# Moving the transposing loads and the output writes of a feed-forward stage from ScalarE's DMA queue to SyncE's

## The reference

```python
# attention-like part: a gated linear scan
params = einsum('btc,dc->btd', x, W) + b
gates, values = split(params, 2, axis=-1)
_, hidden = associative_scan(lambda a, b: (b.g*a.g, b.g*a.v + b.v),
                             (sigmoid(gates), tanh(values)), axis=1)
# feed-forward part, weights made ternary: {-1, 0, 1} * mean|w|
h = square(relu(einsum('bsd,hd->bsh', x, ternarize(w_fc))))   # H = 5120
y = einsum('bsh,dh->bsd', h, ternarize(w_proj))               # D = 2048
# the layer
x = x + layernorm(scan_part(layernorm(x)))
x = x + layernorm(ffn_part(layernorm(x)))
```

## Time and profile before

| | us |
|---|---|
| median of the 2 runs shown | 5565.78 |
| the two runs | 5473.66 and 5657.90 |
| the profiled execution, device time | 5452.77 |
| the profiled execution, span of the slowest core (core 2) | 5451.2 |
| spans of the eight cores | 5438.5 to 5451.2 |
| TensorE busy with matmuls, core 2 | 3681.0 (68%) |
| ScalarE busy | 1327.7 (24%) |
| VectorE busy | 1291.4 (24%) |
| GpSimd busy | 101.2 (2%) |

### The profile page before, as it was taken

The page is one execution under the profiler, slowest core; times in us unless marked ns, Lnnn a source line. Parts: engine busy times, 40 slices in busy tenths (PEclk is TensorE's granted clock), DMA queues, the critical chain, the costliest instruction groups (busy, mean ns, idle before and its releaser), DMA issues.

```text
span 5451.2 us, 57166 instructions; the slowest of 8 cores (5438.5 to 5451.2 us)
## 1 busy us (share of the span) xinstructions
PE 3681.0 (68%) x20742; PEld 2111.9 (39%) x20742; DVE 1291.4 (24%) x1830; ACT 1327.7 (24%) x2801; POOL 101.2 (2%) x140
## 2 busy tenths in 40 slices
PE   0004656068888889332695994986959949869897
PEld 0001222067777778331242442432424424324343
DVE  0466555022222322565002002011020020110101
ACT  0004666123333332000211302213113022131221
POOL 0000011000000000000000000000000000000000
PEclk9999999999999999655797996988979979989898
DMA  9787775722222221797445445444454454444443
GB/s 122 227 298 256 259 271 221 159 95 90 93 94 95 89 94 60 261 312 266 154 152 195 146 151 174 150 166 165 151 196 148 151 172 153 172 162 153 172 151 143
DMA packets 314431, 918.22 MB, mean 168 GB/s; under 512 B 220848, under 2 KB 220976, under 8 KB 229168
## 3 DMA queue, kind: packets, MB, share of 16 engines
q1 hardware_dynamic: 204976, 604.16, 32.4%
q0 software_dynamic: 21632, 192.95, 11.5%
q10 hardware_dynamic: 87552, 117.46, 6.5%
HBM read 704.76 MB, written 192.94 MB: 165 GB/s over the span
## 4 chain that ended last, share of the span: by engine, by line
PE 59%; DMA 11%; DVE 10%; ACT 7%; issue 5%; ACTq 3%; another core or an unknown queue 2%; SPq 2%; DVEq 0%; POOLq 0%
PE ps_pj L902 20%; PE ps_fc L889 20%; PE ps_par L550 15%; DMA x_sb<-x 4%; ACTq L811 3%; DMA wslab<-wfc 3%; DVE st6c L46 3%; DMA wslab<-wpj 2%; PE ps_bf L353 2%; ACT stage_pj L374 2%; PE ps_bf L345 2%; ACT stage_fc L367 1%; DMA x1a_sb<-x_s 1%; DVE st6a L46 1%
## 5 line engine op out<-in xcount | busy, mean ns | idle before, releaser
L889 PE MATMUL ps_fc<-xn1T_sb,sfc_sb 128*128 128x512 bf16 x5120 | 1133.3, 385 | 436.2 <-ACT r_sb L823 351.1
L550 PE MATMUL ps_par<-xnT_sb,wt_sb 128*128 128x256 bf16 x8192 | 935.1, 279 | 293.4 <-ACT g_sb L520 148.2
L902 PE MATMUL ps_pj<-hfc_sb,spj_sb 128*128 128x512 bf16 x5120 | 1106.9, 379 | 15.4 <-ACT hfc_sb L827 15.3
L550 PEld LDWEIGHTS ps_par<-xnT_sb,wt_sb 128*128 128x128 bf16 x8192 | 818.7, 100 | 409.6 <-issue 297.3
L889 PEld LDWEIGHTS ps_fc<-xn1T_sb,sfc_sb 128*128 128x128 bf16 x5120 | 505.5, 99 | 1061.7 <-issue 477.4
L902 PEld LDWEIGHTS ps_pj<-hfc_sb,spj_sb 128*128 128x128 bf16 x5120 | 500.1, 98 | 622.2 <-issue 21.0
L46 DVE BATCH_NORM_STATS2 st6c<-ps_yT 128x6 f32<-128x512 bf16 x128 | 79.7, 685 | 2391.5 <-PE ps_yT L913 2390.8
L823 ACT ACTIVATE r_sb<-ps_fc,am_fc 128x512 f32<-128x512 f32 x320 | 219.9, 687 | 807.0 <-PE ps_fc L889 633.8
L835 ACT CAST y_sb<-ps_pj 128x512 bf16<-128x512 f32 x128 | 75.0, 586 | 1040.3 <-PE ps_pj L902 1040.3
L476 DVE TENSOR_TENSOR_SCAN h_sb<-g_sb,carry,v_sb 128x256 f32<-128x256 f32 x224 | 168.2, 751 | 611.1 <-ACT v_sb L526 593.1
L224 PE MATMUL ps_misc<-id_sb,red 128*1 128x128 f32 x1 | 0.4, 372 | 454.4 <-DVE red L217 454.4
(11 more groups left out here) (76 smaller groups left out, 1598.2 us busy)
## 6 DMA issues: line engine op xcount, KB each, us to landing
sfc_sb<-sfcT_t SPq DMA_DIRECT2D x160, 1024.0 KB, 5.0
spj_sb<-spjT_t SPq DMA_DIRECT2D x128, 1280.0 KB, 6.6
wslab<-wfc SPq DMA_DIRECT2D x80, 1024.0 KB, 5.5
wslab<-wpj SPq DMA_DIRECT2D x32, 2560.0 KB, 10.5
x_sb<-x SPq DMA_DIRECT2D x16, 2048.0 KB, 8.1
h_t<-h_sb POOLq DMA_DIRECT2D x16, 2048.0 KB, 6.6
x_sb<-x ACTq DMA_DIRECT2D x16, 2048.0 KB, 11.3
htin_sb<-h_t SPq DMA_DIRECT2D x16, 2048.0 KB, 13.7
```

The lines of the kernel that those rows point to most:

```text
L550: ins = tensor.matmul(pp[:, 0:CH1], wt_sb[:, ct, col0:col0 + 128], xnT_sb[:, k % 3, ct, :], start=(ct == 0), stop=(ct == NC - 1))
L889: ins = tensor.matmul(ps_fc[gh % 2][:, 0:CH2], sfc_sb[:, ghb % 2, ct, (ht % 2) * 128:(ht % 2 + 1) * 128], xn1T_sb[:, q % 2, ct, :], start= ...
L902: ins = tensor.matmul(ps_pj[gc % 2][:, 0:CH2], spj_sb[:, gc % 2, ht, :], hfc_sb[:, ht, :], start=(ht == 0), stop=(ht == NH - 1))
```

## The change

In the last stage, the function xn1T_seg and its calls are taken out of ScalarE's block, and so are the output write behind v_o8 and the final wait for the writes. SP's block takes both over. For each chunk q SP now does, in this order: wait for the chunk's xn1 rows and for fc of chunk q - 2; issue the sixteen DMA transposes of chunk q; for q of 1 or more, wait for v_o8 and issue the output write for each of the four tiles of chunk q - 1; then the sfc_sb and spj_sb loads of chunk q as before. The output writes of the last chunk and the final wait stand at the end. The wait for d_x1w7 (x1 written) at SP's start is taken out. Buffers, tile sizes, the computation and the other engines' blocks stay as they are.

```diff
--- before.py
+++ after.py
@@ ScalarE @@
-                    def xn1T_seg(scalar, q):
-                        if q == 0:
-                            rwait_all(scalar, d_sw, NHB + NC)
-                        rwait_all(scalar, d_xn1w, TT2 * (q + 1))
-                        _w(scalar, p_fc, NH * (q - 1))
-                        for ct in range(NC):
-                            scalar.dma_start(
-                                out=xn1T_sb[:, q % 2, ct, :],
-                                in_=xn1_d[q * CH2:(q + 1) * CH2, ct * 128:(ct + 1) * 128],
-                                transpose=True).then_inc(d_xn1T[q % 2], 16)
-
                     def comp_seg(scalar, q):
-                        if q + 1 < NQ:
-                            xn1T_seg(scalar, q + 1)
                         for ht in range(NH):
...
                                 scale=sceff[:, 0:1]).then_inc(g_xp8, 1)
-                            scalar.wait_ge(v_o8, gq + 1)
-                            rinc(scalar.dma_start(out=out_rows[gq],
-                                             in_=out2_sb[:, gq % 2, :]), d_out8, gq)
 
                     ln3s_seg(scalar, 0)
-                    xn1T_seg(scalar, 0)
...
                     comp_seg(scalar, NQ - 1)
-                    rwait_all(scalar, d_out8, NT128)
@@ SP @@
                     for q in range(NQ):
                         if q == 0:
                             rwait_all(sync, d_sw, NHB + NC)
-                            rwait_all(sync, d_x1w7, NCH)
+                        rwait_all(sync, d_xn1w, TT2 * (q + 1))
+                        _w(sync, p_fc, NH * (q - 1))
+                        for ct in range(NC):
+                            sync.dma_start(
+                                out=xn1T_sb[:, q % 2, ct, :],
+                                in_=xn1_d[q * CH2:(q + 1) * CH2, ct * 128:(ct + 1) * 128],
+                                transpose=True).then_inc(d_xn1T[q % 2], 16)
+                        if q >= 1:
+                            for tt in range(TT2):
+                                gq = (q - 1) * TT2 + tt
+                                sync.wait_ge(v_o8, gq + 1)
+                                rinc(sync.dma_start(out=out_rows[gq],
+                                                 in_=out2_sb[:, gq % 2, :]), d_out8, gq)
                         for hb in range(NHB):
...
+                    for tt in range(TT2):
+                        gq = (NQ - 1) * TT2 + tt
+                        sync.wait_ge(v_o8, gq + 1)
+                        rinc(sync.dma_start(out=out_rows[gq],
+                                         in_=out2_sb[:, gq % 2, :]), d_out8, gq)
+                    rwait_all(sync, d_out8, NT128)
```

## The result

Against the kernel before on the same chip, the changed kernel takes 0.976 of the time (95% interval 0.972 to 0.980). The profiled execution took 5319.0 us against 5452.8: 133.8 us less, where 151 were forecast. The medians over all executions are 5643.67 us (11 runs, 5304 to 5859) and 5717.24 us (10 runs, 5447 to 5954); in many executions of both kernels some cores ran at a lower granted clock and took up to 550 us longer, so that the medians can't be compared with the profile and the ratio leaves such executions out.

The account below looks back on a forecast made before the run. ScalarE's order between chunks, which makes TensorE wait, was taken as the bound. Gains of 140.6 and 31.9 less 6 and 15.5 make 151 us, so 5452.8 becomes 5302 us; range 5268 to 5400 (5280 to 5325 at 0.70).

Parts of the forecast that it names:

- What bounds the kernel: Last stage, between chunks: TensorE waits 351.1 us for ScalarE's evacuation, which stands behind layernorm and sixteen DMA transposes ScalarE issues.
- 1.4 us from the last xn1b activation to the third group at six boundaries: Chunks 0/1 to 5/6: transposes off ScalarE cut this interval from 24.8 us to about 1.4; 140.6 us gained.
- The weights' new place: sfc loads behind output writes on SP: 8 us landing, hidden by xn1b at six boundaries, 15.5 us lost at the last.
- 1 us each for x1a: Six boundaries: the third x1a load slows beside the sfc pair, between 0 and 2.8 us each; 6 us lost in all.
- Nothing for SP's transposes beside spj_sb: During projection: SP's transposes follow the last spj_sb load and cost 0; bound 20 us over seven boundaries.
- The start of the stage: Chunk 0: ScalarE freed of transposes, TensorE starts 3.6 us later but its third group sooner; 31.9 us gained (27 to 34).
- The absolute time: Whole kernel: 5452.8 us of the profiled execution less 151 gives 5302 us; range 5268 to 5400.
- rival 1: Six boundaries: x1a loads grow to 15.3 us, costing 36 us in place of 6; 5332 us, chance 0.13.
- rivals 2 and 3: At the boundaries: weights last everywhere, 5379 us, chance 0.05; landing so late the kernel slows, 5650 us, chance 0.02.
- rival 4: Six boundaries: TensorE's clock stays up after the shorter pause, 15 us in all; 5281 us with x1a free, chance 0.08.
- Faster by over 2%: Whole kernel: gain of 2.8 per cent forecast; chance 0.91 of faster by over two per cent (109 us).

Follow-up runs that it names:

- The removal of the cover: Changed kernel, but ScalarE normalises the next chunk's tiles between its copies of pj instead of between the chunks; ratio 0.960 to the kernel before.

## Why the prediction was right or wrong, point by point

- *What bounds the kernel.* Right: ScalarE's order between the chunks. With the next chunk's layernorm taken out of it as well, and no late weights, chunk to chunk takes another 25 us less (315.8 against 340.8): 29.7 less at the boundary and 4.7 more in pj.
- *1.4 us from the last xn1b activation to the third group at six boundaries.* Right: 1.40 us at each of them on six cores, 1.8 on two. Chunk to chunk 21.9 us were gained where 22.4 were forecast.
- *The weights' new place.* Right in size and in kind. For the landing 8 us were taken, and 8.6 measured as a mean of the eight cores at the last boundary. The weights are hidden at six boundaries and cost 15.1 us at the last (15.5 forecast). The removal of the cover, and of the late weights after it, shows both.
- *1 us each for x1a.* Right: 1.1 us, by the kernel with the writes given back. The 1 us was picked between 0 and 2.8, so the hit is in part luck: with the first weight load just ahead of the write instead of behind it, it is 1.6 us more.
- *Nothing for SP's transposes beside spj_sb.* Right: TensorE's busy time and waits in pj are unchanged, 129.4 us from the first to the last copy against 129.5 before.
- *The start of the stage.* This term of the sum failed, 31.9 us. It took the sixteen transposes at the 21.4 us that they had needed in a quiet place, and freed ScalarE at the same time, although it is just this freeing that lets GpSimd's loads of x1a and x1b start beside them. The traffic stretched the transposes to 36.8 us in the mean. The weights, issued behind them, let TensorE start 18.2 us later than before where 3.6 were forecast, and ScalarE's last xn1b activation of chunk 1 came 14.5 us sooner instead of 19.5. So 19.8 us were gained instead of 31.9, outside the 27 to 34 given for the term (10.8 on core 4, the slowest, between the two profiles). The prediction named more traffic for the six boundaries and not for the place with the most of it.
- *The absolute time.* This is the step that put the forecast outside its own range. The sum set out from the 5452.8 us of one profiled execution, and the range, 5268 to 5400, took in only part of the scatter of the two runs shown, 5473.66 and 5657.90. It holds the profiled execution, 5319.0 us, but not the median of 5643.67. An exact gain would not have helped: the kernel before has a median of 5717.24 over ten executions, and 151 less than that is 5566. The difference could be forecast from the profile; the time that it is taken from could not.
- *The rivals.* x1a grew by 1 us, not 6 (rival 1). The weights came last only where forecast (rivals 2 and 3). TensorE did not stay warm (rival 4): after its pause of 9.61 us the granted clock was 0.52 in the next six us, as it was in the kernel before after 53.35 us, and 1.00 in the six us after that in both.
- *Faster by over 2%.* So it is on the measured ratio, though by 2.4% and not 2.8%, and the interval's upper end is just at 2%.

## What to carry to other kernels

Read an engine's order at the place where it is last, and move out of it what has another place: here a layernorm and sixteen DMA issues fitted into 8 us gaps of the same engine and gave 5.7%, where moving the issues to another queue gave 2.4%. A load that is put behind a late wait on a shared queue costs nothing as long as something else is later, and comes due at every round once that is repaired; so note what covers it. And when a wait goes away, ask what the freed engine had been holding back, for those transfers now run beside the ones that you timed in quiet.

## What the runs showed of the hardware

- DMA transposes became slower beside other transfers, and so did the other transfers. The transposes of chunk 0, sixteen that fill 128x512 bf16 each, took 20.2 to 22.3 us in all when little else ran, whether ScalarE or SP issued them, and 31.8 to 49.7 us beside 4 MB of GpSimd's loads (three kernels), single ones up to 12 us; an x1a load took 25.6 us there. What in the DMA engines does this, no run here tells.
- With a 1 MB weight load in flight on the other queue, the time from the issue of a 512 KB write to the first transpose behind it was 5.6 us instead of 3.0 (means of eight cores and six boundaries). No run isolates the load.
- A weight load issued ahead of a 1 MB write on the same queue landed 1.8 us sooner than one issued behind it (6.8 against 8.6 us, eight cores each).
- After a pause of TensorE of 9.61 us, as after one of 53.35 us, the granted clock of the next six us was 0.52, about the lower of its two levels (1.2 and 2.4 GHz), and 1.00 in the six us after that.
